# Last layer normalisation of a decoder layer: ten of 32 row tiles scaled on GpSimd and VectorE, not on ScalarE

## The chip, the cores and the metric

One core of one Trainium2 chip. The time is the device time of the whole program in microseconds (us), the median of the runs. Rows and columns below are those of SBUF tiles: 128 partitions, and so many float32 values in each.

## What is computed

A decoder layer with three residual blocks, each followed by a layer normalisation without gain or offset, for 16 batches of 256 tokens with 256 features:

```
_layernorm(x): m = mean(x, -1); v = var(x, -1); return (x - m) / sqrt(v + 1e-5)
x = _layernorm(x + state_space_mixer(x))
x = _layernorm(x + cross_attention(ctx_1024, x))
x = _layernorm(x + mixture_of_8_experts(x))
```

The change touches the last of the three `_layernorm` alone: 4096 tokens, each reduced over its 256 features to a mean and a variance, then scaled.

## The kernel before, in words

The program has two parts. The first runs over the batches and their heads (projections, attention, routing), and scatters the routed tokens into `slots` in memory. The second runs over the eight experts: `slots` is read, two matrix products are made, and GpSimd adds the results with indirect DMAs into `accd` in memory, which already holds the tokens themselves (`add`, line 2058).

When the last of these adds has landed, the final normalisation begins. Its tokens come as 32 row tiles (FN = 32) of 128 partitions and 256 columns in the tile `fx`, in LC = 12 groups. `FR = [1, 1, 2] + [4] * 6 + [2, 1, 1]` (line 268) gives the rows of each group, `FO` the first row. The engines work on the groups as a chain, each with its instructions in program order, and only semaphores between them:

- SP issues all 12 loads `fx <- accd` (line 587), each with its own semaphore `part_ld[c]`. Then, in the order of the groups, it waits for `fy_set` and issues the store `out <- fx` (line 590), and at last waits for all stores.
- VectorE (lines 1829 to 1848), in iteration c: `bn_stats` of each row of group c (1834); then, for the group before it, `f_nm` = -mean * rs (1840), which waits for GpSimd's `frs_set`; then `bn_aggr` of each row of group c (1845) and `f_vv` = variance + epsilon (1848). Each of the last two waits for the one ahead of it through `fstat_set`.
- GpSimd (lines 2066 to 2068), for each group: waits for `f_vv` and raises it to the power -0.5 into `f_rs`, one `tensor_tensor` of 128 partitions and as many columns as the group has rows. `frs_set` counts these.
- ScalarE (lines 1277 to 1282), for each group: waits for `fnm_set`, then scales each row in place, `fx = fx * rs + nm`, one activation a row; the last one adds to `fy_set`.

GpSimd's `tensor_scalar` with subtract and multiply, both operands one value for each partition, is also at lines 1878 (`cxn`), 1907 (`x1`) and 1983 (`xrow`), all of 128 partitions and 256 columns; at 1953 (`prob`) it has one such operand and a constant, for 333 columns. VectorE's same form is at 1740 (`xrow_b`).

Of the kernel before, what the change touches and what calls it, by code (L numbers as in the profile page):

```python
# [22 lines left out]
ALU = mybir.AluOpType  # L23
# [65 lines left out]
def build(nc, x, xT, ctxt, in_w, xp_w, out_w, vecs, vec16, Wq, Wkv, Wo, bo, emb, W1, W2, out):  # L89
# [8 lines left out]
    with top:  # L98
        def sb(name, shape, dt=F32, where=top):
            return where.enter_context(nc.sbuf_tensor(name, shape, dt))  # L100

        def sem(name):
            return top.enter_context(nc.semaphore(name))
# [26 lines left out]
        w2_lo0 = sb("w2_lo0", [P, I // P * D], F32R)  # L130
        xsl0 = sb("xsl0", [P, ST, ROW])
        assert sum(int(np.prod(shape[1:])) for _, shape in MIXER) <= 2 * KD * I + 2 * I // P * D + ST * ROW


# [108 lines left out]
        def s2(name, shape, dt=F32):  # L243
            return sb(name, shape, dt, two)
# [8 lines left out]
        def weights_in(e):  # L253
# [14 lines left out]
        FR = [1, 1, 2] + [4] * 6 + [2, 1, 1]  # L268
        LC, FN = len(FR), sum(FR)
        FO = [sum(FR[:c]) for c in range(LC)]  # L270
        assert FN * P == NTOK
        fx = s2("fx", [P, FN, D])
        f_st = s2("f_st", [P, FN, 6])
        f_mv = s2("f_mv", [P, FN, 2])
        f_vv = s2("f_vv", [P, FN])
        f_rs = s2("f_rs", [P, FN])
        f_nm = s2("f_nm", [P, FN])
# [56 lines left out]
        fstat_set, frs_set, fnm_set, fy_set, out_st = (  # L334
            sem("fstat_set"), sem("frs_set"),
            sem("fnm_set"), sem("fy_set"), sem("out_st"))
# [59 lines left out]
        def ap(t):  # L396
            return t.bitcast(F32)
# [34 lines left out]
        def _(sp):  # L432
# [150 lines left out]
            def rows_of(d, c):  # L583
                return d[P * FO[c]:P * (FO[c] + FR[c]), :].rearrange("(p r) d -> p r d", p=P)
# [1 line left out]
            for c in range(LC):  # L586
                sp.dma_start(fx[:, FO[c]:FO[c] + FR[c], :], rows_of(accd, c)).then_inc(part_ld[c], 16)
            for c in range(LC):
                sp.wait_ge(fy_set, c + 1)
                sp.dma_start(rows_of(out, c), fx[:, FO[c]:FO[c] + FR[c], :]).then_inc(out_st, 16)  # L590
            sp.wait_ge(out_st, 16 * LC)

# [381 lines left out]
        def _(act):  # L974
# [118 lines left out]
            def split_hi(chunks):  # L1093
                for c in chunks:
                    _, which, half = CHUNKS[c]
                    act.wait_ge(part_ld[c], 16)
                    act.activation(w_hi[:, which, 1024 * half:1024 * (half + 1)], staged(c),
                                   ACT.Copy, scale=1.0 if which else QSCALE).then_inc(w_hi_set, 1)
# [176 lines left out]


            for c in range(LC):
                act.wait_ge(fnm_set, c + 1)
                for r in range(FO[c], FO[c] + FR[c]):
                    last = act.activation(fx[:, r, :], fx[:, r, :], IDN, bias=f_nm[:, r:r + 1],  # L1280
                                          scale=f_rs[:, r:r + 1])
                last.then_inc(fy_set, 1)
# [3 lines left out]
        def _(dve):  # L1286
# [273 lines left out]
            def split_lo(chunks):  # L1560
                for c in chunks:
                    _, which, half = CHUNKS[c]
                    o = (slice(None), which, slice(1024 * half, 1024 * (half + 1)))
                    dve.wait_ge(w_hi_set, c + 1)
                    dve.scalar_tensor_tensor(out=w_lo[o], in0=staged(c), scalar=1.0 if which else QSCALE,
                                             in1=ap(w_hi[o]), op0=ALU.mult, op1=ALU.subtract).then_inc(w_lo_set, 1)
# [254 lines left out]
            for half in range(2):  # L1821
                for i in range(I // P):
# [3 lines left out]
                                             in1=ap(h_hi[:, i, o]), op0=ALU.max, op1=ALU.subtract).then_inc(hl_set, 1)  # L1826


            for c in range(LC + 1):
                if c < LC:  # L1830
                    own = slice(FO[c], FO[c] + FR[c])
                    dve.wait_ge(part_ld[c], 32)
                    for r in range(FO[c], FO[c] + FR[c]):
                        last = dve.bn_stats(f_st[:, r, :], fx[:, r, :])
                    last.then_inc(fstat_set, 1)
                if c:

                    old = slice(FO[c - 1], FO[c - 1] + FR[c - 1])
                    dve.wait_ge(frs_set, c)
                    dve.scalar_tensor_tensor(out=f_nm[:, old], in0=f_mv[:, old, 0], scalar=-1.0,  # L1840
                                             in1=f_rs[:, old], op0=ALU.mult, op1=ALU.mult).then_inc(fnm_set, 1)
                if c < LC:
                    dve.wait_ge(fstat_set, 3 * c + 1)
                    for r in range(FO[c], FO[c] + FR[c]):
                        last = dve.bn_aggr(f_mv[:, r, :], f_st[:, r, :])
                    last.then_inc(fstat_set, 1)
                    dve.wait_ge(fstat_set, 3 * c + 2)
                    dve.tensor_scalar(f_vv[:, own], f_mv[:, own, 1], EPS, None, ALU.add).then_inc(fstat_set, 1)
# [3 lines left out]
        def _(pool):  # L1852
# [62 lines left out]
            def split_lo(chunks):  # L1915
                for c in chunks:
                    _, which, half = CHUNKS[c]
                    o = (slice(None), which, slice(1024 * half, 1024 * (half + 1)))
                    pool.wait_ge(w_hi_set, c + 1)
                    pool.tensor_tensor(w_lo[o], staged(c), ap(w_hi[o]), ALU.subtract).then_inc(wk_lo_set, 1)  # L1920
# [145 lines left out]
            for c in range(LC):  # L2066
                pool.wait_ge(fstat_set, 3 * c + 3)
                pool.tensor_tensor(f_rs[:, FO[c]:FO[c] + FR[c]], f_vv[:, FO[c]:FO[c] + FR[c]], powm[:, 0:FR[c]], ALU.pow).then_inc(frs_set, 1)


# [49 lines left out]
```

## Time and profile before

| | |
|---|---|
| runs | 1036.82 us median of 3 (1035.61 to 1037.85) |
| the profiled execution | 1040.01 us, its span 1038.3 us |
| busy in the span: PE, DVE, ACT, POOL | 979.4, 810.6, 729.3, 568.4 us |
| from the first load of the final normalisation (1010.57) to the end | 27.7 us |
| ACT, 32 scalings of a row (line 1280) | 16.1 us |
| DVE, 32 `bn_stats` (line 1834) | 11.6 us |
| POOL, 12 powers (line 2068) | 9.6 us |

PE is TensorE, DVE VectorE, ACT ScalarE, POOL GpSimd, SP SyncE; SPq is SP's queue of DMA issues. Times of single instructions are taken from the profiled execution and counted from the start of its span. An instruction's recorded time includes its way through the engine's pipeline, so two that follow each other overlap, and the distance between their starts is less than the recorded time.

### The profile page before, as it was taken

What the parts mean: (1) busy time and instruction counts of PE and PEld (TensorE: products, weight loads), DVE (VectorE), ACT (ScalarE), POOL (GpSimd) and SP (SyncE); (2) the same over time, 40 slices, a digit from 0 to 9 for tenths busy, and PEclk for the clock granted to TensorE, in tenths of its full rate; (3) what the DMA queues carried; (4) which work ended last, traced back from release to release, by engine and by line L of the source; (5) the groups of instructions that cost most, each with busy time, mean ns of one, the idle gap of its engine ahead of it and who ended that gap; (6) DMA issues with size and microseconds to landing.
All of it is one profiled execution on the core that took longest, in us unless ns stands there. A gap on an engine that the chain in (4) does not pass through costs nothing.

```text
span 1038.3 us, 21394 instructions
## 1 busy us (share of the span) xinstructions
PE 979.4 (94%) x6977; PEld 928.9 (89%) x6977; DVE 810.6 (78%) x2042; ACT 729.3 (70%) x1865; POOL 568.4 (55%) x964
## 2 busy tenths in 40 slices
PE   6899999999999999999999999999999999899960
PEld 4799999999999999999999999999999999799960
DVE  7777888888888888888888888878887877555526
ACT  5677767777777768776878787768786766355536
POOL 4544455565565546564656456545655454446543
PEclk9899999999999999999999999999999999999985
DMA  7462031112111131113110411041105111755448
GB/s 244 163 181 97 25 104 48 49 46 90 62 50 45 58 94 51 45 53 100 51 45 17 135 50 45 18 135 49 46 11 172 29 41 44 298 133 88 66 54 317
DMA packets 63829, 89.60 MB, mean 86 GB/s; under 512 B 14932, under 2 KB 44680, under 8 KB 63720
## 3 DMA queue, kind: packets, MB, share of 16 engines
q1 hardware_dynamic: 56040, 75.51, 22.4%
q0 software_dynamic: 7680, 12.72, 5.7%
q8 instruction: 58, 0.95, 0.4%
q14 instruction: 51, 0.42, 0.1%
HBM read 49.21 MB, written 38.99 MB: 85 GB/s over the span
## 4 chain that ended last, share of the span: by engine, by line
PE 78%; ACT 8%; DVE 6%; issue 3%; DMA 2%; POOL 1%; SPq 0%; ACTq 0%; DVEq 0%; POOLq 0%
PE ps L598 21%; PE ps L599 20%; PE ps L600 20%; PE ps L626 7%; PE ps L705 3%; DVE nmx L1714 1%; ACT fx L1280 1%; PE ps L643 1%; PE ps L641 1%; PE ps L743 1%; ACT hp L1003 1%; ACT ys_x L1104 1%; ACT prob L1162 1%; PE ps L736 1%; POOL accd L2058 1%
## 5 line engine op out<-in xcount | busy, mean ns | idle before, releaser
L1953 POOL TENSOR_SCALAR prob<-prob,rinv 128x333 f32<-128x333 f32 x256 | 144.5, 575 | 248.3 <-DVE rinv L1723 247.3
L1157 ACT ACTIVATE oT_hi<-ps 128x256 fp32r<-128x256 f32 x128 | 49.3, 385 | 156.6 <-PE ps L643 156.6
L598 PE MATMUL ps<-kv_lo,w_hi 128*128 128x256 f32 (+1 forms) x512 | 155.5, 304 | 0.6 <-DVE kv_lo L1288 0.6
L600 PE MATMUL ps<-kv_hi,w_hi 128*128 128x256 f32 (+1 forms) x512 | 154.5, 302 | 0.0
L599 PE MATMUL ps<-kv_hi,w_lo 128*128 128x256 f32 (+1 forms) x512 | 154.1, 301 | 0.0
L1162 ACT ACTIVATE prob<-ps,nmx 128x333 f32<-128x333 f32 x256 | 135.0, 538 | 7.6 <-DVE nmx L1714 7.6
L1288 DVE TENSOR_TENSOR pT_lo<-ps,pT_hi 128x512 fp32r<-128x512 f32 (+1 forms) x256 | 133.1, 550 | 1.8 <-ACT pT_hi L1174 0.6
L1714 DVE TENSOR_REDUCE nmx<-ps 128x2 f32<-128x666 f32 x128 | 108.3, 846 | 9.7 <-PE ps L600 9.0
L626 PE MATMUL ps<-ident,prob 128*128 128x128 f32 (+1 forms) x768 | 105.7, 273 | 1.8 <-DVE oT_lo L1288 1.6
L598 PEld LDWEIGHTS ps<-kv_lo,w_hi 128*128 128x128 f32 x512 | 98.1, 192 | 1.4 <-issue 1.3
L599 PEld LDWEIGHTS ps<-kv_hi,w_lo 128*128 128x128 f32 x512 | 97.5, 190 | 0.0
L600 PEld LDWEIGHTS ps<-kv_hi,w_hi 128*128 128x128 f32 x512 | 97.5, 190 | 0.0
L626 PEld LDWEIGHTS ps<-ident,prob 128*128 128x128 f32 (+1 forms) x768 | 90.2, 139 | 6.3 <-issue 2.8
L1349 DVE SCALAR_TENSOR_TENSOR cv<-hp,vec,cv 128x256 f32<-128x256 f32 x192 | 87.6, 475 | 1.1 <-ACT cv L1051 1.1
L598 PE MATMUL ps<-k_lo,q_hi 128*128 128x334 f32 x256 | 81.2, 317 | 3.4 <-DVE k_lo L1294 3.4
L1294 DVE SCALAR_TENSOR_TENSOR k_lo<-ps,vec,k_hi 128x334 fp32r<-128x334 f32 x128 | 71.6, 559 | 13.5 <-ACT k_hi L982 13.1
L599 PE MATMUL ps<-k_hi,q_lo 128*128 128x334 f32 x256 | 81.1, 317 | 0.0
L600 PE MATMUL ps<-k_hi,q_hi 128*128 128x334 f32 x256 | 80.9, 316 | 0.0
L598 PE MATMUL ps<-w_lo,oT_hi 128*128 128x256 f32 x256 | 78.6, 307 | 0.9 <-DVE oT_lo L1288 0.9
L1174 ACT ACTIVATE pT_hi<-ps 128x512 fp32r<-128x512 f32 x128 | 77.6, 607 | 0.5
L2058 POOL DMA_INDIRECT accd<-yo,tku x32 | 53.4, 1669 | 44.9 <-ACT yo L1221 34.7
L1302 DVE SCALAR_TENSOR_TENSOR q_lo<-ps,vec,q_hi 128x256 fp32r<-128x256 f32 x128 | 55.8, 477 | 26.7 <-ACT q_hi L990 26.6
(272 smaller groups left out, 3281.9 us busy)
## 6 DMA issues: line engine op xcount, KB each, us to landing
wraw<-in_W SPq DMA_DIRECT2D x14, 512.0 KB, 7.0
vcd_hi<-vst_hi SPq DMA_DIRECT2D x10, 512.0 KB, 2.8
vcd_lo<-vst_lo SPq DMA_DIRECT2D x10, 512.0 KB, 3.8
v_hi<-vcd_hi SPq DMA_DIRECT2D x32, 154.0 KB
v_lo<-vcd_hi SPq DMA_DIRECT2D x32, 154.0 KB
slots<-initr SPq DMA_DIRECT2D x8, 520.0 KB, 7.7
xs<-in_x SPq DMA_DIRECT2D x16, 256.0 KB, 4.2
xts<-in_xT SPq DMA_DIRECT2D x15, 256.0 KB, 4.1
```

The lines of the kernel that those rows point to most:

```text
L598: pe.matmul(dst, hi1, lo2, start=first, stop=False, skip_group_check=True)
L599: pe.matmul(dst, lo1, hi2, start=False, stop=False, skip_group_check=True)
L600: return pe.matmul(dst, hi1, hi2, start=False, stop=last, skip_group_check=True)
L626: last = pe.transpose(ps[0:r, T0 + j // 2, (j % 2) * S + t * P:(j % 2) * S + t * P + P], prob[:, ring, t, j * P:j * P + r], ident[:])
L1162: act.activation(prob[:, h % 2, t, 0:KEYS], ps[:, S0 + t, 0:KEYS], ACT.Exp, bias=nmx[:, h % 2, t:t + 1], accum_out=rsum[:, h % 2, t:t + 1] ...
L1174: act.activation(pT_hi[:, 0:2, :].rearrange("p j s -> p (j s)"), ps[:, T0, :], ACT.Copy).then_inc(pTh_set, 1)
L1288: return dve.tensor_tensor(dst, src, ap(hi), ALU.subtract)
L1294: dve.scalar_tensor_tensor(out=k_lo[:, idx % 2, :], in0=g[:, 0:KCOL], scalar=vec[:, V_BK + idx:V_BK + idx + 1], in1=ap(k_hi[:, idx % 2, :] ...
L1349: op = dve.scalar_tensor_tensor(out=cv[:, ct, :], in0=hp[:, ct, k:k + S], scalar=w, in1=cv[:, ct, :], op0=ALU.mult, op1=ALU.add)
L1714: dve.tensor_reduce(nmx[:, h % 2, :], ps[:, S0:S0 + NT, 0:KEYS], AX.X, ALU.max, negate=True).then_inc(nmx_set, 1)
L1953: pool.tensor_scalar(prob[:, h % 2, t, 0:KEYS], prob[:, h % 2, t, 0:KEYS], rinv[:, h % 2, t:t + 1], 1.0, ALU.mult, ALU.mult).then_inc(norm ...
L2058: pool.indirect_dma_start(accd, bass.IndirectOffsetOnAxis(tku[u][:, s:s + 1], 0), yo[u][:, s, :], None, compute_op=ALU.add).then_inc(add_d ...
```

## The change

Of every group with four rows, the last row is scaled by GpSimd, behind the group's power, with `tensor_scalar` (subtract the mean, multiply by rs); ScalarE scales the other three. The rows of the last three groups (2, 1, 1) are scaled by VectorE with the same form in place of `f_nm`, and ScalarE leaves these groups out. GpSimd waits on `frs_set` for its own power before it scales, and counts its scaled row on the same semaphore, so the numbers that the others wait for become tables: `RS_AT[c]` is the count at which group c's rs is there, `NM_AT[c]` that of its `f_nm` (or its scaled rows). SP waits, for a group of four, for `fy_set` and for GpSimd's row; for the last three groups for `fnm_set`.

```
+        BY_POOL = [int(n == 4) for n in FR]
+        BY_DVE = [int(n < 4 and c > LC // 2) for c, n in enumerate(FR)]
+        RS_AT = [1 + c + sum(BY_POOL[:c]) for c in range(LC)]
+        NM_AT = [1 + c for c in range(LC)]
...
             for c in range(LC):
-                sp.wait_ge(fy_set, c + 1)
+                if BY_DVE[c]:
+                    sp.wait_ge(fnm_set, NM_AT[c])
+                else:
+                    sp.wait_ge(fy_set, c + 1)
+                if BY_POOL[c]:
+                    sp.wait_ge(frs_set, RS_AT[c] + 1)
                 sp.dma_start(rows_of(out, c), fx[:, FO[c]:FO[c] + FR[c], :]).then_inc(out_st, 16)
...
             for c in range(LC):
-                act.wait_ge(fnm_set, c + 1)
-                for r in range(FO[c], FO[c] + FR[c]):
+                if BY_DVE[c]:
+                    continue
+                act.wait_ge(fnm_set, NM_AT[c])
+                for r in range(FO[c], FO[c] + FR[c] - BY_POOL[c]):
                     last = act.activation(fx[:, r, :], fx[:, r, :], IDN, bias=f_nm[:, r:r + 1],
                                           scale=f_rs[:, r:r + 1])
...
-                    dve.wait_ge(frs_set, c)
-                    dve.scalar_tensor_tensor(out=f_nm[:, old], in0=f_mv[:, old, 0], scalar=-1.0,
-                                             in1=f_rs[:, old], op0=ALU.mult, op1=ALU.mult).then_inc(fnm_set, 1)
+                    dve.wait_ge(frs_set, RS_AT[c - 1])
+                    if BY_DVE[c - 1]:
+                        for r in range(FO[c - 1], FO[c - 1] + FR[c - 1]):
+                            last = dve.tensor_scalar(fx[:, r, :], fx[:, r, :], f_mv[:, r, 0:1], f_rs[:, r:r + 1],
+                                                     ALU.subtract, ALU.mult)
+                        last.then_inc(fnm_set, 1)
+                    else:
+                        dve.scalar_tensor_tensor(out=f_nm[:, old], in0=f_mv[:, old, 0], scalar=-1.0,
+                                                 in1=f_rs[:, old], op0=ALU.mult, op1=ALU.mult).then_inc(fnm_set, 1)
...
                 pool.tensor_tensor(f_rs[:, FO[c]:FO[c] + FR[c]], f_vv[:, FO[c]:FO[c] + FR[c]], powm[:, 0:FR[c]], ALU.pow).then_inc(frs_set, 1)
+                if BY_POOL[c]:
+                    r = FO[c] + FR[c] - 1
+                    pool.wait_ge(frs_set, RS_AT[c])
+                    pool.tensor_scalar(fx[:, r, :], fx[:, r, :], f_mv[:, r, 0:1], f_rs[:, r:r + 1],
+                                       ALU.subtract, ALU.mult).then_inc(frs_set, 1)
```

GpSimd's instructions of the final normalisation, before (all of them; what an instruction waits for stands in brackets):

```order
L2068 TENSOR_TENSOR f_rs<-f_vv,powm 128x1 [waits fstat_set] x2
L2068 TENSOR_TENSOR f_rs<-f_vv,powm 128x2 [waits fstat_set]
L2068 TENSOR_TENSOR f_rs<-f_vv,powm 128x4 [waits fstat_set] x6
L2068 TENSOR_TENSOR f_rs<-f_vv,powm 128x2 [waits fstat_set]
L2068 TENSOR_TENSOR f_rs<-f_vv,powm 128x1 [waits fstat_set] x2
```

and with the change, from the same place up to the third group of four:

```order
L2085 TENSOR_TENSOR f_rs<-f_vv,powm 128x1 [waits fstat_set] x2
L2085 TENSOR_TENSOR f_rs<-f_vv,powm 128x2 [waits fstat_set]
L2085 TENSOR_TENSOR f_rs<-f_vv,powm 128x4 [waits fstat_set]
L2089 TENSOR_SCALAR fx<-fx,f_mv,f_rs 128x256 [waits frs_set]
L2085 TENSOR_TENSOR f_rs<-f_vv,powm 128x4 [waits fstat_set]
L2089 TENSOR_SCALAR fx<-fx,f_mv,f_rs 128x256 [waits frs_set]
L2085 TENSOR_TENSOR f_rs<-f_vv,powm 128x4 [waits fstat_set]
L2089 TENSOR_SCALAR fx<-fx,f_mv,f_rs 128x256 [waits frs_set]
L2085 TENSOR_TENSOR f_rs<-f_vv,powm 128x4 [waits fstat_set]
```

Behind each power of four columns now stands a scaling of a row of 256, and the next group's power behind that.

VectorE's last nine instructions before, from the statistics of the second last group on:

```order
L1834 BN_STATS f_st<-fx 128x6 [waits xpr_ld]
L1840 SCALAR_TENSOR_TENSOR f_nm<-f_mv,f_rs 128x2 [waits frs_set]
L1845 BN_AGGR f_mv<-f_st 128x2 [waits fstat_set]
L1848 TENSOR_SCALAR f_vv<-f_mv 128x1 [waits fstat_set]
L1834 BN_STATS f_st<-fx 128x6 [waits xT1_ld]
L1840 SCALAR_TENSOR_TENSOR f_nm<-f_mv,f_rs 128x1 [waits frs_set]
L1845 BN_AGGR f_mv<-f_st 128x2 [waits fstat_set]
L1848 TENSOR_SCALAR f_vv<-f_mv 128x1 [waits fstat_set]
L1840 SCALAR_TENSOR_TENSOR f_nm<-f_mv,f_rs 128x1 [waits frs_set]
```

and with the change its last ten:

```order
L1845 BN_STATS f_st<-fx 128x6 [waits xpr_ld]
L1853 TENSOR_SCALAR fx<-fx,f_mv,f_rs 128x256 [waits frs_set]
L1853 TENSOR_SCALAR fx<-fx,f_mv,f_rs 128x256
L1862 BN_AGGR f_mv<-f_st 128x2 [waits fstat_set]
L1865 TENSOR_SCALAR f_vv<-f_mv 128x1 [waits fstat_set]
L1845 BN_STATS f_st<-fx 128x6 [waits xT1_ld]
L1853 TENSOR_SCALAR fx<-fx,f_mv,f_rs 128x256 [waits frs_set]
L1862 BN_AGGR f_mv<-f_st 128x2 [waits fstat_set]
L1865 TENSOR_SCALAR f_vv<-f_mv 128x1 [waits fstat_set]
L1853 TENSOR_SCALAR fx<-fx,f_mv,f_rs 128x256 [waits frs_set]
```

Each `f_nm` of the last three groups has become one or two scalings at the same place, ahead of the aggregates of the next group.

## Rows read from the trace of the kernel before

**Rows 1.** The page: busy time of each engine.
```profile
PE 979.4 (94%) x6977; PEld 928.9 (89%) x6977; DVE 810.6 (78%) x2042; ACT 729.3 (70%) x1865; POOL 568.4 (55%) x964
```

**Rows 2.** The chain of waits from 1016 us: start us, us, what.
```profile
1011.89 4.53 DMA fx<-accd
...
1016.44 1.41 DVE f_st L1834 x4
...
1019.87 13.37 ACT fx L1280 x27
```

**Rows 3.** Order of time, first groups of four: start us, us, engine, line; idle before.
```profile
1018.54 1.02 POOL L2068 TENSOR_TENSOR f_rs<-f_vv,powm 128x4 f32<-128x4 f32 x1 [1.38 <-DVE f_vv L1848]
1019.69 0.14 DVE L1840 SCALAR_TENSOR_TENSOR f_nm<-f_mv,f_rs 128x4 f32<-128x4 f32 x1
...
1019.87 13.86 ACT L1280 ACTIVATE fx<-fx,f_nm,f_rs 128x256 f32<-128x256 f32 x28 [0.84 <-DVE f_nm L1840]
...
1020.47 1.01 POOL L2068 TENSOR_TENSOR f_rs<-f_vv,powm 128x4 f32<-128x4 f32 x1 [0.91 <-DVE f_vv L1848]
```

**Rows 4.** Order of time, the last groups on VectorE and GpSimd.
```profile
1028.16 1.01 POOL L2068 TENSOR_TENSOR f_rs<-f_vv,powm 128x4 f32<-128x4 f32 x1 [0.92 <-DVE f_vv L1848]
1029.20 0.16 DVE L1840 SCALAR_TENSOR_TENSOR f_nm<-f_mv,f_rs 128x4 f32<-128x4 f32 x1 [0.47 <-POOL f_rs L2068]
...
1029.80 0.70 POOL L2068 TENSOR_TENSOR f_rs<-f_vv,powm 128x2 f32<-128x2 f32 x1 [0.64 <-DVE f_vv L1848]
1030.53 0.16 DVE L1840 SCALAR_TENSOR_TENSOR f_nm<-f_mv,f_rs 128x2 f32<-128x2 f32 x1 [0.48 <-POOL f_rs L2068]
1030.61 0.17 DVE L1845 BATCH_NORM_AGGREGATE f_mv<-f_st 128x2 f32<-128x6 f32 x1
...
1032.74 0.16 DVE L1840 SCALAR_TENSOR_TENSOR f_nm<-f_mv,f_rs 128x1 f32<-128x1 f32 x1 [0.67 <-POOL f_rs L2068]
```

**Rows 5.** Ten us of the stage: us, busy of PE, PEld, DVE, ACT, POOL; clock, DMA, GB/s.
```profile
1018.00:1028.00 10.00, 0.00 (x0) 0.00 (x0) 9.79 (x56) 9.16 (x19) 5.04 (x5) 0.50 1.04 391
```

**Rows 6.** The output stores from 1031 us on, by the tile fx.
```profile
L590 SPq DMA_DIRECT2D out<-fx x4: 332/335/351, 1031.8 to 1033.8; - x4
...
DMA to landing us min/median/max: 2.1/2.3/2.6
```

**Rows 7.** GpSimd's TENSOR_SCALAR: two lines (ns min/median/max), a group (mean ns), a pair.
```profile
L1907 POOL TENSOR_SCALAR x<-xa,a_mv,a_rs x32: 1208/1218/2440, 34.2 to 828.7; 128x256 f32<-128x256 f32 x32
L1983 POOL TENSOR_SCALAR xrow<-xb,c_mv,c_rs x30: 1207/1222/1494, 122.7 to 867.3; 128x256 f32<-128x256 f32 x30
L1953 POOL TENSOR_SCALAR prob<-prob,rinv 128x333 f32<-128x333 f32 x256 | 144.5, 575 | 248.3 <-DVE rinv L1723 247.3
296.68 2.42 POOL L1907 TENSOR_SCALAR x<-xa,a_mv,a_rs 128x256 f32<-128x256 f32 x2
```

**Rows 8.** Order of time on GpSimd, a power and the scaling that waits for it.
```profile
7.34 0.55 POOL L1875 TENSOR_TENSOR x_rs<-x_vv,powm 128x1 f32<-128x1 f32 x1 [5.42 <-DVE x_vv L1384]
8.00 1.52 POOL L1878 TENSOR_SCALAR cxn<-cxs,x_mv,x_rs 128x256 f32<-128x256 f32 x1
```

**Rows 9.** VectorE's TENSOR_SCALAR of the same form: the line, and its two instructions.
```profile
L1740 DVE TENSOR_SCALAR xrow_b<-xb,c_mv,c_rs x2: 407/410/414, 895.6 to 895.9; 128x256 f32<-128x256 f32 x2
895.56 0.74 DVE L1740 TENSOR_SCALAR xrow_b<-xb,c_mv,c_rs 128x256 f32<-128x256 f32 x2 [0.84 <-POOL c_rs L1973]
```

**Rows 10.** Order of time where VectorE reads two SBUF tensors beside such scalings.
```profile
298.57 0.19 DVE L1404 TENSOR_TENSOR mask<-iota,idxf 128x32 f32<-128x32 f32 x1
...
335.31 0.41 DVE L1412 SCALAR_TENSOR_TENSOR gt<-th,ut 16x256 f32<-16x256 f32 x1 [0.80 <-ACT th L1010]
...
335.43 2.61 POOL L1983 TENSOR_SCALAR xrow<-xb,c_mv,c_rs 128x256 f32<-128x256 f32 x2 [0.21 <-POOL c_rs L1973]
...
349.65 2.42 POOL L1907 TENSOR_SCALAR x<-xa,a_mv,a_rs 128x256 f32<-128x256 f32 x2
...
350.93 0.52 DVE L1404 TENSOR_TENSOR mask<-iota,idxf 128x32 f32<-128x32 f32 x1
```

## Prediction

> **What bounds the kernel now.** I read the page's busy times first, then the chain of waits that ends last, then the order of time of the last 28 us, and at the end single groups of instructions for prices. TensorE is busy for 94% of the span [rows 1], but the change touches nothing before the end of the last expert's scatter-add, and TensorE has no work behind that (0.00 of the 10 us of [rows 5]). What counts is the stretch that runs from 1010.6 us to the end, 1038.3.
>
> There the chain goes through the first loads, then VectorE's statistics of the first group of four, and from 1019.87 on through 27 ScalarE scalings without a break [rows 2]. So ScalarE looks like the limit, and the change takes rows from it. But the reader should look at who is just behind it. One group of four costs ScalarE 4 x 0.495 = 1.98 us (13.86 us for 28 rows [rows 3]). The rhythm of the groups is 1.92 us: from GpSimd's power for the first group of four at 1018.54 to that of the sixth at 1028.16 it is 9.62 us for five groups [rows 3, 4], and it is VectorE's rhythm, for VectorE is busy for 9.79 of 10 us [rows 5]. Taking work from ScalarE alone could therefore not shorten a group by more than 0.06 us. At the end ScalarE runs 0.83 us behind VectorE's last f_nm (1032.74 + 0.16 to 1019.87 + 13.86 = 1033.73 [rows 4, 3]). GpSimd does one power of 1.01 us for each group and idles 0.92 [rows 4]. Behind the last scaling (1033.73) come a store of 2.1 us [rows 6] and, up to 1038.3, 2.4 us of closing, both taken as fixed.
>
> **The change part by part.**
>
> *Six rows move from ScalarE to GpSimd* (the last row of each group of four), the last four rows to VectorE. ScalarE loses 10 x 0.495 = 4.95 us; it was behind VectorE by less than 1 us, so at most that could be got back.
>
> *GpSimd gets six scalings.* This form (subtract, multiply, both operands one value per partition, 128x256) stands elsewhere in the kernel: medians of two lines 1.22 us, shortest 1.21, and two in a row take 2.42, so it is the spacing too and not only the recorded length [rows 7]. The form with one such operand costs 0.575 for 333 columns, less than half; it is not what is added here. Before the scaling GpSimd now waits for its own power. The only such hand-over with an idle engine took 0.11 us (7.34 + 0.55 = 7.89, next at 8.00 [rows 8]). So GpSimd's work for one group becomes 1.01 + 0.11 + 1.21 + 0.05 (between the scaling and the next power; an estimate between 0, the pair of rows 7, and the 0.11) = **2.38 us, and that is more than VectorE's 1.92.** The cover of 0.92 us idle time is too short by 0.46. GpSimd becomes the bound of the stage. Its queue holds power, scaling, power, scaling: the next group's power stands behind a scaling that nobody urgently needs, VectorE's f_nm waits for that power, and behind f_nm on VectorE wait the aggregates of the group after it. ScalarE, with three rows (1.49 us), is then far from the limit.
>
> The loop starts as before with the power at 1018.54. The sixth power starts 5 x 2.38 = 11.90 later, at 1030.44 instead of 1028.16: +2.28. Its scaling holds the two-row group's power back by one full period more: 1032.82 instead of 1029.80 [rows 4], **+3.02**.
>
> *VectorE scales the last three groups (2, 1, 1 rows)* where it computed f_nm. Its price for this form is 0.41 a row, and 0.74 for two, so 0.33 apart [rows 9]. From the two-row power to the last f_nm there are now 1032.74 - 1029.80 = 2.94 us, with three waits for powers in them [rows 4]. The two-row f_nm took 0.08 of this up to the next instruction (1030.53 to 1030.61) and becomes two scalings with 0.66: +0.58. The one-row f_nm behind it becomes 0.33: +0.25. At the end stands a scaling of 0.41. That is 4.18 us. Before, ScalarE ended 1033.73 - 1029.80 = 3.93 after that power. So this part costs **+0.25** itself: ScalarE's backlog was hidden behind the same waits that VectorE now sits through with longer instructions.
>
> *SP* now waits for frs_set or fnm_set, too. Group stores need GpSimd's row at power + 1.33 and ScalarE's at power + 0.03 + 0.18 (f_nm to the first scaling, [rows 3]) + 1.58 = 1.8, so the added wait is passed already: nothing. The last store is alone on its queue then; the shortest of the last four takes 2.1 us now [rows 6], and I leave it at that: nothing saved. *DMA:* the middle of the stage runs at 391 GB/s with all 16 DMA engines busy [rows 5], but the chain has VectorE released by a load for the last time at 1016.41, for the first group of four [rows 2]; a slower rhythm asks less of it.
>
> Sum: 3.02 + 0.25 = +3.27 us on the profiled execution's 1040.01, so 1043.3. That one is 3.2 above the median 1036.82, of which nothing lies in this stage that I can see, so I put the difference on the median: 1036.82 + 3.27 = **1040.1 us**.
>
> Bounds. Below: own hand-over 0.03 as between engines [rows 4], none behind the scaling: 2.25 a group, six times 13.5, the two-row power at 1032.04, +2.24 + 0.25 = +2.5. Above: the scaling stretched. Beside VectorE instructions with two SBUF inputs of 256 columns it took 1.40 to 1.49 [rows 7, 10]; at 1.40 and 0.11 on both sides it is 2.63 a group: +4.5 + 0.25 = +4.8. In this stage only f_nm has two SBUF inputs, and it has four columns, so I stay at 1.21.
>
> **What the skill says against the row.** The rows say 1.21 us for 256 columns of one input. The Trainium skill (GPSIMD Engine Reference, Engine selection) says that one-input elementwise work runs on GpSimd at roughly line rate. By it the scaling would be short and hidden, and the sum +0.25 us; that is rival 1. No row of this kernel with two per-partition operands agrees.
>
> **Rivals.**
>
> *1. The scaling fits into GpSimd's gap: no change.* If it cost what the one-operand form costs, 0.575 x 256 / 333 = 0.44 us, the group would be 1.01 + 0.11 + 0.44 = 1.56, under 1.92; the powers stay where they are, and only the +0.25 of the tail is left: 1037.1. It decides from 1.92 - 1.12 = 0.80 us down. For it: the short form in rows 7. Against it: 62 instructions of the same form, none under 1.20. The same would be seen if the row did not reach GpSimd, but its order shows it there. Chance 8%.
>
> *2. GpSimd's row locks VectorE's f_nm out.* f_nm reads two SBUF tensors; it is due 0.03 us after the power, 0.08 before the row. If it had to wait for the row's end, the group would be a ring: 1.01 + 0.11 + 1.21 + 0.03, then from f_nm to the next power 0.78 (1019.69 to 1020.47 [rows 3]): 3.14 us. Five of them put the sixth power at 1034.24, f_nm behind it at 1036.60, the two-row power 0.60 later at 1037.20 (1029.20 to 1029.80 [rows 4]), the end 4.18 later at 1041.38: +7.65, or 1044.5. Against it: a VectorE instruction with two SBUF inputs ran 0.52 us, not over 1.2, beside such a row, at another place 0.19 [rows 7, 10]. Chance 5%. The Trainium skill (SBUF — State Buffer, SBUF: two separate sides) has such a rule: GpSimd and a VectorE instruction with two SBUF inputs share ports that one holds for a whole instruction. By it this rival is right where the row comes first, 1044.5; where f_nm comes first, nothing changes. Rows 10 show something milder than a lock for the whole row.
>
> *3. The row is stretched to 1.4 us* by VectorE: +4.8 as worked out, 1041.6. Chance 7%, at the edge of the range.
>
> **How the numbers follow.** GpSimd's 2.38 us as the bound: 78%; with rivals 3 and 2, 90% for slower. No measurement of this kernel tells 0.2% (2.07 us) from no change; the sum is 1.2 above that line, the bound below 0.4 above it, and medians of three move by about 1 us (1035.61 to 1037.85), so I give 0.07 of this back: slower 0.83. Same 0.14 (rival 1 and the rest). Faster 0.03: no step wins 2 us, as VectorE's 1.92 stands. Range: below +2.5 less 1.0 for the median, 1038.3; above it reaches to rival 3, with a rest for the median, 1041.9; rivals 1 and 2 are outside.
>
> **What would show it.** Right: GpSimd's powers of four columns 2.3 to 2.5 us apart with no idle time between them, its scalings at 1.21; VectorE idle before f_nm for some 0.4 us a group, released by the power; ScalarE idle about 0.9 a group; the chain of waits on GpSimd from 1018.5 to 1033; the last store issued about 1037. Wrong: scalings under 0.8 us with powers still 1.92 apart (rival 1); f_nm starting behind the scaling's end, powers 3.1 apart (rival 2); scalings at 1.4 (rival 3).

## The result

The changed kernel takes 1040.55 us (median of 6 runs, 1040.30 to 1042.16), the kernel before 1037.34 us beside it (6 runs, 1035.61 to 1040.29). The ratio is 1.0032, with a 95% interval of 1.0022 to 1.0042: slower by 3.3 us, 2.3 to 4.4. The forecast was 1040.1 us, slower by 3.27.

### The profile after

The page's line of busy times, which answers to [rows 1]:

```profile
PE 978.2 (94%) x6977; PEld 927.4 (89%) x6977; DVE 812.0 (78%) x2043; ACT 725.0 (70%) x1855; POOL 577.3 (56%) x970
```

ScalarE lost ten instructions and 4.3 us, GpSimd gained six and 8.9 us. This span is 1038.8 us, only 0.5 longer than before; the first load of the stage was issued at 1007.85 here and at 1010.57 there, since everything ahead of the stage took 2.7 us more in the profiled execution of the kernel before. The stage itself is compared, not the span.

Order of time, one group of four in the middle of the stage (answers to [rows 3]):

```profile
1022.51 1.03 POOL L2085 TENSOR_TENSOR f_rs<-f_vv,powm 128x4 f32<-128x4 f32 x1
1023.58 0.17 DVE L1857 SCALAR_TENSOR_TENSOR f_nm<-f_mv,f_rs 128x4 f32<-128x4 f32 x1 [0.36 <-POOL f_rs L2085]
1023.65 1.23 POOL L2089 TENSOR_SCALAR fx<-fx,f_mv,f_rs 128x256 f32<-128x256 f32 x1
...
1023.78 1.58 ACT L1291 ACTIVATE fx<-fx,f_nm,f_rs 128x256 f32<-128x256 f32 x3 [0.75 <-DVE f_nm L1857]
1024.07 0.17 DVE L1865 TENSOR_SCALAR f_vv<-f_mv 128x4 f32<-128x4 f32 x1
...
1024.84 1.03 POOL L2085 TENSOR_TENSOR f_rs<-f_vv,powm 128x4 f32<-128x4 f32 x1
```

GpSimd's rows have no bracket here: from the scaling of the second group of four to the power of the two-row group it never waits for another engine. Its power and its scaling fill the 2.33 us from one power to the next, VectorE stands 0.36 us before f_nm until the power is there, and ScalarE 0.75 us before its three rows. Before the change a power started 0.25 us behind the start of its f_vv; at that distance the power of the next group could start at 1024.07 + 0.25 = 1024.32, and it starts at 1024.84, when the scaling is done.

The first interval was another: 2.78 us, since VectorE's statistics there waited 0.75 us for a load (1015.72), and GpSimd then 0.42 us for f_vv.

The chain of waits has moved to GpSimd (answers to [rows 2]; start us, us, what):

```profile
1022.55 1.01 POOL f_rs L2085
1023.56 0.09 issue
1023.65 1.23 POOL fx L2089
1024.88 1.01 POOL f_rs L2085
```

This view ends with the scaling of the last row, at 1033.7, as it ended with ScalarE's last scaling before. What lies between that and the end of the program it does not show; that comes below.

The last groups (answers to [rows 4]):

```profile
1029.50 0.72 POOL L2085 TENSOR_TENSOR f_rs<-f_vv,powm 128x2 f32<-128x2 f32 x1
1030.26 0.73 DVE L1853 TENSOR_SCALAR fx<-fx,f_mv,f_rs 128x256 f32<-128x256 f32 x2 [1.05 <-POOL f_rs L2085]
...
1031.35 0.55 POOL L2085 TENSOR_TENSOR f_rs<-f_vv,powm 128x1 f32<-128x1 f32 x1 [1.13 <-DVE f_vv L1865]
1031.93 0.41 DVE L1853 TENSOR_SCALAR fx<-fx,f_mv,f_rs 128x256 f32<-128x256 f32 x1 [0.33 <-POOL f_rs L2085]
...
1032.70 0.56 POOL L2085 TENSOR_TENSOR f_rs<-f_vv,powm 128x1 f32<-128x1 f32 x1 [0.81 <-DVE f_vv L1865]
1033.30 0.41 DVE L1853 TENSOR_SCALAR fx<-fx,f_mv,f_rs 128x256 f32<-128x256 f32 x1 [0.67 <-POOL f_rs L2085]
```

Here the roles turn: GpSimd waits for VectorE, 1.13 and 0.81 us, where it waited 0.56 and 0.55 before, because VectorE now scales rows of 256 columns ahead of the f_vv that the next power needs. From the two-row power to the last one it is 3.20 us; before, it was 2.35.

### What ends the program

The forecast let the program end a fixed time behind the last store. An instruction that each engine runs at its very end, on the line of the program's block (98), says otherwise. It is a DRAIN. ScalarE's ends 0.04 us and VectorE's 0.05 us behind the end of that engine's last instruction, so it is a wait for the engine's own work; GpSimd's goes on for 5.3 us more. The rows give count, ns (min/median/max) and the time of the start. Of the kernel before:

```profile
L98 POOLq DRAIN  x1: 5913/5913/5913, 1032.1 to 1032.1; - x1
...
L98 SPq DRAIN  x1: 7/7/7, 1036.1 to 1036.1; - x1
```

and of the changed kernel:

```profile
L98 POOLq DRAIN  x1: 5913/5913/5913, 1032.7 to 1032.7; - x1
...
L98 SPq DRAIN  x1: 7/7/7, 1035.6 to 1035.6; - x1
```

SP is past its wait for the last store at 1036.1 before, 2.2 us ahead of the end, and at 1035.6 after, 3.2 us ahead of it. GpSimd's DRAIN starts beside its last power and takes 5.91 us, to 1038.0 and 1038.6, and 0.2 us behind its end the program is over (1038.3, 1038.8). So the last store has 2 us to spare before and 3 after, and by these rows the time is set by the end of GpSimd's last instruction, with 5.55 us behind it; the experiment with spare powers below puts it to the test. What stood in the code as the last step, the scaling of the last row, is off the path; the last power, with the 5.3 us of DRAIN behind it, is on it. In these terms the stage took, from the first load's issue to the end of the last power, 22.1 us before (1010.57 to 1032.70) and 25.4 us after (1007.85 to 1033.26): +3.3. That this is just what the runs measured is partly chance. Up to the first power of four columns the kernel before took 8.0 us and the changed one 7.2, for loads that landed sooner or later; from there to the two-row power it is +3.19, and from that to the last power +0.85. Against a second profile of the kernel before (below, 21.45 us) the same count gives +4.0.

### The profile page after: what moved, and what is told of

Its sections match the earlier page's. It is cut to its first block, busy times and chain, and to the rows that moved or that the text cites. A ratio compares the mean times of both kernels' runs of the same rounds, so it can differ in the third digit from the quotient of the medians.

```text
span 1038.8 us, 21397 instructions
## 1 busy us (share of the span) xinstructions
PE 978.2 (94%) x6977; PEld 927.4 (89%) x6977; DVE 812.0 (78%) x2043; ACT 725.0 (70%) x1855; POOL 577.3 (56%) x970
## 3 DMA queue, kind: packets, MB, share of 16 engines
q1 hardware_dynamic: 56040, 75.51, 22.1%
## 4 chain that ended last, share of the span: by engine, by line
PE 78%; ACT 7%; DVE 6%; issue 4%; POOL 3%; DMA 2%; SPq 0%; POOLq 0%; ACTq 0%; DVEq 0%
PE ps L607 20%; PE ps L608 20%; PE ps L609 20%; PE ps L635 7%; PE ps L714 3%; DVE nmx L1725 1%; POOL accd L2075 1%; PE ps L650 1%; PE ps L652 1%; PE ps L752 1%; ACT hp L1012 1%; ACT ys_x L1113 1%; ACT prob L1171 1%; DMA accd<-yo,tku 1%; PE ps L708 1%
## 5 line engine op out<-in xcount | busy, mean ns | idle before, releaser
L1299 DVE TENSOR_TENSOR oT_lo<-ps,oT_hi 128x256 fp32r<-128x256 f32 x128 | 54.1, 422 | 27.8 <-ACT oT_hi L1166 24.0
```

What stands on the lines that cost most here:

```text
L1299: return dve.tensor_tensor(dst, src, ap(hi), ALU.subtract)
```

## The experiments

Each kernel was timed beside the kernel before on the same chip. The first six take the change apart, the others test the end of the program.

### Only VectorE's part

```
-        BY_POOL = [int(n == 4) for n in FR]
+        BY_POOL = [0 for n in FR]
```

> Only the part on VectorE is kept: the last three groups (2, 1, 1 rows) are scaled by VectorE, GpSimd scales nothing, ScalarE scales all four rows of the groups of four. Theory (GpSimd's work per group is the rhythm): the powers of four columns stay 1.92 us apart, and only the +0.25 us of the tail is left, so within 0.1% of before. Rival (the loss sits in the tail or in the closing behind it): the +3.2 us of the change are still here.

Measured: 1.0009 (1.0000 to 1.0017), +0.9 us. Its last powers in order of time:

```profile
1029.11 0.69 POOL L2085 TENSOR_TENSOR f_rs<-f_vv,powm 128x2 f32<-128x2 f32 x1 [0.64 <-DVE f_vv L1865]
1030.93 0.55 POOL L2085 TENSOR_TENSOR f_rs<-f_vv,powm 128x1 f32<-128x1 f32 x1 [1.13 <-DVE f_vv L1865]
1032.29 0.55 POOL L2085 TENSOR_TENSOR f_rs<-f_vv,powm 128x1 f32<-128x1 f32 x1 [0.81 <-DVE f_vv L1865]
```

From the two-row power to the last it is 3.18 us, not 2.35: +0.83, over three times the +0.25 expected. The time agrees with +0.83, but its interval (0.0 to 1.8 us) holds +0.25 too, so the price is read from the profile; all five profiled kernels that have this tail and no row between its powers show 3.18 to 3.20 us. The +0.25 was counted to the last scaling, which the end of the program does not hang on. The powers of four columns are 1.92 apart but for the first interval of 2.30, where the statistics waited for a load. The +3.2 of the rival lies outside the interval. The tail is a minor part, as the theory had it, but its price was read at the wrong place.

### Only GpSimd's part

```
-        BY_DVE = [int(n < 4 and c > LC // 2) for c, n in enumerate(FR)]
+        BY_DVE = [0 for n in FR]
```

> Only the part on GpSimd is kept: it scales the last row of each group of four, and ScalarE scales the last three groups as before. Theory: powers 2.33 us apart as in the changed kernel's trace; from the first power of four columns to the two-row power 6 x 2.33 = 13.98 instead of 11.26 us, so about +2.7 us over before, 0.25 under the whole change. Rival (tail): no change from before.

Measured: 1.0019 (1.0011 to 1.0028), +2.0 us (1.1 to 2.9). In its profile the powers of four columns lie 2.31 to 2.35 us apart (before: 1.92), and from the first of them to the two-row power it is 13.95 us instead of 11.26, +2.69. The +2.7 lies inside the interval, no change outside. The two parts together, 0.9 + 2.0 = 2.9, account for the whole within their intervals.

### Half a row

```
-                for r in range(FO[c], FO[c] + FR[c] - BY_POOL[c]):
-                    last = act.activation(fx[:, r, :], fx[:, r, :], IDN, bias=f_nm[:, r:r + 1],
+                for r in range(FO[c], FO[c] + FR[c]):
+                    w = 128 if BY_POOL[c] and r == FO[c] + FR[c] - 1 else D
+                    last = act.activation(fx[:, r, 0:w], fx[:, r, 0:w], IDN, bias=f_nm[:, r:r + 1],
...
-                    pool.tensor_scalar(fx[:, r, :], fx[:, r, :], f_mv[:, r, 0:1], f_rs[:, r:r + 1],
+                    pool.tensor_scalar(fx[:, r, 128:D], fx[:, r, 128:D], f_mv[:, r, 0:1], f_rs[:, r:r + 1],
```

> The whole change, but GpSimd scales only the last 128 columns of its row and ScalarE the first 128; same number of instructions and of waits on GpSimd. Theory: a scaling of some 0.6 to 0.7 us makes 1.01 + 0.11 + 0.65 = 1.77 us a group, under VectorE's 1.92, so the powers are 1.92 apart again and the time is that of before +0.3 us. Rival (the extra instruction with its own wait and its place in the queue costs, whatever its length): powers still over 2.1 apart, and +1.5 to +3 us.

Measured: 1.0011 (1.0002 to 1.0020), +1.1 us. GpSimd, order of time:

```profile
1020.69 1.03 POOL L2086 TENSOR_TENSOR f_rs<-f_vv,powm 128x4 f32<-128x4 f32 x1
1021.83 0.80 POOL L2090 TENSOR_SCALAR fx<-fx,f_mv,f_rs 128x128 f32<-128x128 f32 x1
1022.59 1.03 POOL L2086 TENSOR_TENSOR f_rs<-f_vv,powm 128x4 f32<-128x4 f32 x1
```

Half the columns cost 0.80, not the 0.6 to 0.7 expected; the part that does not go with the columns is larger. From the third power of four columns on GpSimd is busy without a gap even so, at 1.90 us a group, and that is just VectorE's rhythm: 0.80 us is also where the prediction put its point of decision. (The first two intervals were 2.54 and 2.07 us, behind a wait of 0.51 us for a load.) What is left over before is the tail: from the two-row power to the last 3.20 us instead of 2.35, and the power of the two-row group 1.90 behind the sixth where it was 1.64, +1.1 together. The interval (0.2 to 2.1 us) still touches what the rival expects, +1.5 to +3, but its other sign, powers over 2.1 apart, is missing wherever VectorE did not wait for a load. Same kinds of instruction, same waits, same queue as the change, but about a third of its cost. The time of the scaling decides, not its being there.

### Two rows

```
-                for r in range(FO[c], FO[c] + FR[c] - BY_POOL[c]):
+                for r in range(FO[c], FO[c] + FR[c] - 2 * BY_POOL[c]):
...
-                    r = FO[c] + FR[c] - 1
+                    r = FO[c] + FR[c] - 2
                     pool.wait_ge(frs_set, RS_AT[c])
                     pool.tensor_scalar(fx[:, r, :], fx[:, r, :], f_mv[:, r, 0:1], f_rs[:, r:r + 1],
+                                       ALU.subtract, ALU.mult)
+                    r = FO[c] + FR[c] - 1
+                    pool.tensor_scalar(fx[:, r, :], fx[:, r, :], f_mv[:, r, 0:1], f_rs[:, r:r + 1],
                                        ALU.subtract, ALU.mult).then_inc(frs_set, 1)
```

> The whole change, but GpSimd scales two rows of each group of four and ScalarE two. Theory: 1.03 + 0.10 + 2 x 1.22 = 3.56 us a group; 6 x 3.56 = 21.4 instead of 11.26, so +10.1, and +0.25 for the tail: +10.3 us over before (1.0%). Rival (the loss is a fixed cost for each group, from waits or from locking out f_nm, not GpSimd's working time): about +3.2 again, or under +6.

Measured: 1.0098 (1.0084 to 1.0113), +10.2 us (8.7 to 11.7).

```profile
1026.47 1.03 POOL L2085 TENSOR_TENSOR f_rs<-f_vv,powm 128x4 f32<-128x4 f32 x1
1027.60 1.22 POOL L2089 TENSOR_SCALAR fx<-fx,f_mv,f_rs 128x256 f32<-128x256 f32 x1
1028.81 1.22 POOL L2092 TENSOR_SCALAR fx<-fx,f_mv,f_rs 128x256 f32<-128x256 f32 x1
1029.99 1.03 POOL L2085 TENSOR_TENSOR f_rs<-f_vv,powm 128x4 f32<-128x4 f32 x1
```

3.52 us a group. The second row adds its full 1.2 us six times, where the first one added only what went beyond the gap of 0.8 (0.92 us of idle time less 0.11 for the wait). That is how a resource behaves that is the bound.

### The row behind the next power

GpSimd scales the row of group c - 1 after the power of group c; the table `RS_AT` and SP's counts follow from it (not shown).

```
-                if BY_POOL[c]:
-                    r = FO[c] + FR[c] - 1
-                    pool.wait_ge(frs_set, RS_AT[c])
+                if c and BY_POOL[c - 1]:
+                    r = FO[c - 1] + FR[c - 1] - 1
+                    pool.wait_ge(frs_set, RS_AT[c - 1])
```

> The whole change, but GpSimd's row of a group stands behind the power of the next group. Theory (GpSimd's working time): it still has 1.01 + 0.03 to 0.1 + 1.22 us for a group, so about 2.25 to 2.33 apart; the two-row power comes some 0.8 us earlier than with the change, since one row fewer stands ahead of it: -0.7 us against the change, still +2.5 over before. Rival (only the place in the queue is at fault: a row ahead of an urgent power): powers 1.92 apart and about +0.9, as with the tail alone.

Measured: 1.0023 (1.0013 to 1.0033), +2.4 us (1.4 to 3.4). The powers lie 2.17 to 2.36 us apart, so the rival (1.92 apart, +0.9) is out. The forecast of 0.7 us less than the change fits, but is not shown: the two intervals overlap. From the first power of four columns to the last power it is 17.0 us here and 17.65 in the changed kernel's profile, where GpSimd stood 0.42 us behind the wait for a load. The place in the queue is worth under 1 us; GpSimd's working time is the rest.

This run shows one more thing, since here the row starts ahead of f_nm:

```profile
1021.60 1.02 POOL L2086 TENSOR_TENSOR f_rs<-f_vv,powm 128x4 f32<-128x4 f32 x1
1022.62 1.23 POOL L2090 TENSOR_SCALAR fx<-fx,f_mv,f_rs 128x256 f32<-128x256 f32 x1
1022.66 0.53 DVE L1858 SCALAR_TENSOR_TENSOR f_nm<-f_mv,f_rs 128x4 f32<-128x4 f32 x1 [0.25 <-POOL f_rs L2086]
...
1023.51 0.36 DVE L1866 TENSOR_SCALAR f_vv<-f_mv 128x4 f32<-128x4 f32 x1
...
1023.96 1.03 POOL L2086 TENSOR_TENSOR f_rs<-f_vv,powm 128x4 f32<-128x4 f32 x1
```

The f_nm that start 0.03 to 0.05 us behind the row take 0.16, 0.53, 0.16 and 0.53 us, where they take 0.14 to 0.16 alone, and f_vv takes up to 0.37 instead of 0.17; the next power then waits 0.11 us for it. Where f_nm is behind the row, VectorE's short instructions are sometimes stretched, but none waited for the row's end.

### One operand for each partition

```
-                    pool.tensor_scalar(fx[:, r, :], fx[:, r, :], f_mv[:, r, 0:1], f_rs[:, r:r + 1],
-                                       ALU.subtract, ALU.mult).then_inc(frs_set, 1)
+                    pool.tensor_scalar(fx[:, r, :], fx[:, r, :], f_rs[:, r:r + 1], 1.0,
+                                       ALU.mult, ALU.mult).then_inc(frs_set, 1)
```

> The whole change, but GpSimd's scaling is multiply by rs and multiply by the constant 1.0 (the mean is not subtracted in six of the 32 row tiles): one operand for each partition in place of two, as on the line that took 0.575 us for 333 columns. Theory: 0.44 us for 256 columns, 1.56 us a group, so powers 1.92 apart and about +0.9 us, like the tail on VectorE alone. Rival (every GpSimd scaling of 256 columns takes 1.2 us): powers 2.33 apart and +3.2.

Measured: 1.0004 (0.9991 to 1.0017), +0.4 us (-0.9 to 1.8): the +0.9 lies inside, the rival's +3.2 outside. In its profile:

```profile
1025.97 0.52 POOL L2089 TENSOR_SCALAR fx<-fx,f_rs 128x256 f32<-128x256 f32 x1
1026.78 1.02 POOL L2085 TENSOR_TENSOR f_rs<-f_vv,powm 128x4 f32<-128x4 f32 x1 [0.28 <-DVE f_vv L1865]
```

0.52 us for the same 256 columns, GpSimd waits for VectorE again, 0.28 us a group, and the powers are 1.92 to 1.93 apart but for one at 2.01. So rival 1 of the prediction was a real case with the other form; what separates them is one instruction form at 0.52 and one at 1.23.

### Spare powers at the end

In the kernel before, three powers of four columns that nobody reads stand behind GpSimd's last one (`spare` is a tile of their own):

```
+            for k in range(3):
+                pool.tensor_tensor(spare[:, k, :], f_vv[:, FN - 4:FN], powm[:], ALU.pow)
```

> The kernel before, with three more powers of four columns on GpSimd behind its last one; nobody reads them, they delay no other engine and no store. Theory (the program's end hangs on GpSimd's last instruction: in six profiles it came 6.10 to 6.11 us after the start of GpSimd's last power, whatever the last store did): 3 x 1.01 = +3.0 us. Rival (the end hangs on the last store, which lands 2.4 us before it, and closing is a fixed time behind it, as the prediction had it): 0.0.

Measured: 1.0022 (1.0013 to 1.0031), +2.3 us (1.3 to 3.2).

```profile
1029.75 0.55 POOL L2069 TENSOR_TENSOR f_rs<-f_vv,powm 128x1 f32<-128x1 f32 x1 [0.56 <-DVE f_vv L1849]
1030.27 2.95 POOL L2071 TENSOR_TENSOR spare<-f_vv,powm 128x4 f32<-128x4 f32 x3
```

```profile
L98 POOLq DRAIN  x1: 8817/8817/8817, 1029.7 to 1029.7; - x1
...
L98 SPq DRAIN  x1: 7/7/7, 1033.6 to 1033.6; - x1
```

The DRAIN grew by 2.9 us, SP had finished at 1033.6, and the end came at 1038.8. Work that no engine and no store waits for made the program longer, and its own length of 2.95 us lies inside the interval. The rival (no change) is out.

### The last groups merged

```
-        FR = [1, 1, 2] + [4] * 6 + [2, 1, 1]
+        FR = [1, 1, 2] + [4] * 7
```

(The list of the loads' semaphores is cut to fit ten groups.)

> The kernel before with the last three groups (2, 1, 1 rows) merged into one of four: GpSimd has ten powers, not twelve, VectorE and ScalarE the same rows. Theory (GpSimd's last instruction decides): the seventh power of four columns starts 1.92 us after the sixth, 2.07 earlier than the last power now, and is 0.46 longer: -1.6 us (-0.15%), although the last store is bigger (512 KB) and leaves at the same time or later. Rival (the last store decides): 512 KB in place of 128 KB at the same moment, +0.4 us or more.

Measured: 0.9982 (0.9972 to 0.9992), -1.9 us; once more in a later comparison, 0.9990 (0.9980 to 1.0001).

```profile
1025.01 1.01 POOL L2068 TENSOR_TENSOR f_rs<-f_vv,powm 128x4 f32<-128x4 f32 x1 [0.92 <-DVE f_vv L1848]
1026.94 1.01 POOL L2068 TENSOR_TENSOR f_rs<-f_vv,powm 128x4 f32<-128x4 f32 x1 [0.92 <-DVE f_vv L1848]
```

```profile
L98 POOLq DRAIN  x1: 6365/6365/6365, 1026.9 to 1026.9; - x1
...
L98 SPq DRAIN  x1: 7/7/7, 1033.4 to 1033.4; - x1
```

The last store is four times as large and lands 2.6 us after its issue, not 2.1, and yet the program is shorter; the rival's +0.4 or more is out. GpSimd's DRAIN ends at 1033.3 and SP is through at 1033.4: the two ends now meet, and the program is over at 1033.6.

### The merged group shared

On top of the merge (the wait that SP gets for VectorE's rows is not shown):

```
-                for r in range(FO[c], FO[c] + FR[c]):
+                for r in range(FO[c], FO[c] + FR[c] - 2 * (c == LC - 1)):
...
+                    if c == LC:
+                        for r in range(FN - 2, FN):
+                            last = dve.tensor_scalar(fx[:, r, :], fx[:, r, :], f_mv[:, r, 0:1], f_rs[:, r:r + 1],
+                                                     ALU.subtract, ALU.mult)
+                        last.then_inc(fnm_set, 1)
```

> The kernel with the last three groups merged into one of four rows, and of this last group VectorE scales two rows and ScalarE two, side by side. Theory (the end is the later of two: GpSimd's last instruction + 5.55 us, and the last store's landing + 0.4; in the merged kernel they are 0.13 us apart): the last scaling and the store come about 0.9 us earlier, the end only some 0.1 us: like the merged kernel, -0.2% against before. Rival (the last store decides in the merged kernel): -0.9 us more, -0.27% against before.

> The merged kernel once more, beside the last one on the same chip. Theory and rival expect what they did before: -0.15% against the kernel before; against the shared one, 0 by the theory, +0.9 us by the rival.

Measured, on one chip: shared 0.9991 (0.9982 to 1.0000), merged 0.9990 (0.9980 to 1.0001); medians 1035.45 and 1035.16 us. No gain is seen, but single runs of one kernel scatter over 3 to 5 us here, and the times alone hardly exclude the rival's 0.9 us. The profiles are clearer. The shared kernel's last scaling ends 2.67 us behind its last power's start instead of 3.65, and SP is through at 1032.8, but GpSimd's DRAIN still ends at 1033.3 and the program at 1033.5. In the merged kernel SP was the later of the two by 0.13 us, and that is all that the earlier store can give back. For the size of the merge two measurements stand, -1.9 and -1.0 us, with overlapping intervals; that it is a gain the first shows, the second only makes likely.

### The kernel before, again

> The kernel before, unchanged, for a second profile. Theory: its end comes 5.55 us after the end of GpSimd's last power again, and about 22 us lie between the first load's issue and that power's end (22.14 in the first profile); what else differs between the two profiles is how far apart two executions of one kernel lie. Rival (the closing is a fixed time behind the last store's landing): 2.40 us between that landing and the end again.

```profile
L98 POOLq DRAIN  x1: 5912/5912/5912, 1029.5 to 1029.5; - x1
...
L98 SPq DRAIN  x1: 7/7/7, 1033.4 to 1033.4; - x1
```

The last power ends at 1030.05, the program at 1035.6: 5.55 us again. Its last store landed 2.42 us ahead of the end, much as in the first profile, so this run alone does not tell the two apart. The profiles side by side do:

| kernel | GpSimd's last instruction ends | SP's DRAIN | end | end - GpSimd | end - SP |
|---|---|---|---|---|---|
| before | 1032.70 | 1036.1 | 1038.3 | 5.55 | 2.2 |
| changed | 1033.26 | 1035.6 | 1038.8 | 5.55 | 3.2 |
| VectorE's part | 1032.84 | 1035.3 | 1038.4 | 5.55 | 3.1 |
| two rows | 1040.79 | 1043.2 | 1046.3 | 5.55 | 3.1 |
| spare powers | 1033.22 | 1033.6 | 1038.8 | 5.54 | 5.2 |
| shared | 1027.99 | 1032.8 | 1033.5 | 5.55 | 0.7 |
| merged | 1027.95 | 1033.4 | 1033.6 | 5.68 | 0.2 |

Of the profiles that are not in the table, five have 5.55 us between GpSimd's last instruction and the end too, and the merged kernel's second has 5.70, with SP again 0.2 us ahead of the end. So GpSimd's distance is the same in all but the merged kernels, where SP is through 0.1 to 0.2 us behind GpSimd's DRAIN; SP's is not. All 13 fit one rule: the program ends 0.2 us behind the later of the two DRAINs. From the first load's issue to the last power's end this second profile has 21.45 us, the first 22.14: single executions differ by some 0.7 us in this stage, mostly in when the fourth load lands (5.1 and 5.8 us after the first issue), which is nearly as much as the tail's whole effect of 0.83. That is why one profile is read for intervals between instructions, and the time from many runs.

## Why the prediction was right, and where it was not

**GpSimd becomes the bound, 2.38 us a group: right.** Measured 2.33. The power is 1.03 (1.01 assumed), the wait for its own power 0.10 to 0.11 (0.11), the scaling 1.23 (1.21), and behind the scaling nothing is lost, it even overlaps the next power by 0.04, where 0.05 of loss was assumed: that was the excess. Over six groups the term was sized +3.02; with 2.33 it is 6 x 2.33 - 11.26 = +2.72, and the kernel with this part alone shows 2.69. In the changed kernel's own profile it was +3.19, since the second power of four columns came 2.78 behind the first: the statistics there waited 0.75 us for a load. The prediction had the last wait for a load one group earlier; in several of the profiles, with the change and without, it falls on this second group of four.

**The tail costs +0.25: wrong by a factor of three,** and the step that failed is "behind the last scaling come a store of 2.1 us and 2.4 us of closing, both taken as fixed". The closing is not behind the store. It is GpSimd's DRAIN, which ends 5.3 us behind GpSimd's last power, and it was there in the trace of before, on a line that the prediction does not read. The tail counts up to the last power, and up to there VectorE's scalings add (0.66 - 0.08) + (0.33 - 0.08) = +0.83. The prediction's sum went on to the last scaling, and set VectorE's 0.41 us behind the last f_nm against ScalarE's 0.99, a gain of 0.58 on work that was never on the path. The step's own working had both numbers; it added them up to the wrong end.

**The sum +3.27 against +3.3: right partly by luck.** +0.30 too much in the rhythm stands against 0.6 too little in the tail. With the measured terms it is 2.72 + 0.83 = +3.55, inside the interval of 2.3 to 4.4 as well; the times of the runs do not tell the two sums apart. The profiled execution of before, 3.2 us above the median, also had a part of this in the stage, where the prediction saw none: 0.7 us against its second profile.

**Rival 1 (the scaling fits the gap)** was rightly set aside, and its point of decision, 0.80 us, agrees with the half row. The rule weighed there, the Trainium skill's GPSIMD Engine Reference in Engine selection, that one-input work is roughly line rate, does not hold for this form: 1.23 us for 256 columns and 0.80 for 128, so 0.43 us for each 128 columns and 0.37 beside them.

**Rival 2 (f_nm locked out)** did not happen: f_nm starts 0.04 us behind the power and 0.07 ahead of the row, and takes 0.16 to 0.17. Once both started at the same moment (1018.97), and f_nm took 0.15; once f_nm started 0.86 behind the row's start (1017.04), and took 0.14. So the change is mostly the case in which f_nm comes first and nothing changes. The row comes first in the run with the row behind the next power: there f_nm took up to 0.53 us, but ended 0.66 ahead of the row. The lock for a whole instruction in the Trainium skill's SBUF — State Buffer, SBUF: two separate sides, is not what these traces show for an f_nm of four columns; longer ones were not tried in this stage.

**Rival 3 (the row stretched to 1.4)** did not happen: 1.227 to 1.253.

**SP's added waits: nothing, right.** ScalarE's last row of a group came last, about 0.5 us behind GpSimd's (1025.36 and 1024.88 in the group shown), so SP found the added count reached. **ScalarE's lost rows bring nothing: right,** it stood idle 0.75 us a group.

## What to carry to other kernels

Idle time of an engine is cover only for what fits into it: compare the added instruction, in its exact form, with the idle time for each round of the loop, not with the engine's busy share (55%). Before a last stage is summed up, look at the closing instructions of every engine: the program ends behind the latest of them, and that need not be the engine that does the last useful work. Here the small last groups, which let the last store be small, delayed GpSimd's last power; merging them gained 1 to 2 us, where every sharing of rows that was tried cost time or gained nothing beside it.

## What the runs showed of the hardware

- GpSimd's closing DRAIN ends 5.3 us behind the end of its last instruction in all 13 profiles (5.91 us long with a power of one column, 6.36 with one of four, 8.82 with three more); VectorE's and ScalarE's end 0.03 to 0.05 us behind theirs, and SP's takes 0.01. Whether its length hangs on the indirect DMAs that GpSimd issued before was not tried.
- GpSimd's tensor_scalar of 128x256: 1.23 us with two operands for each partition (subtract, multiply), 0.52 with one and a constant (multiply, multiply). Which of the two, operand or operation, makes the difference was not separated. With 128 columns the first form takes 0.80.
- A VectorE scalar_tensor_tensor of four columns (f_nm) that starts 0.03 to 0.05 us behind such a GpSimd row took 0.53 us twice and 0.16 twice; started ahead of the row or with it, 0.15 to 0.17.
- GpSimd's power costs 0.55, 0.70 and 1.01 us for 1, 2 and 4 columns: some 0.15 us a column.
